# Row maxima per bank with one exponential moved last, another order in the last two steps, and the outputs' transposes taken half by half

## What is computed

```
q    = rmsnorm(rope(h @ Wq_c @ Wq_up)) ; k_sw = rmsnorm(rope(h @ Wk)) ; v_sw = h @ Wv
ck   = rmsnorm(h in blocks of 16 tokens @ W_comp)         # compressed keys, also the values
c    = softmax([mask(q ck / sqrt(D)), sink]) @ ck          # over the blocks that have ended
sw   = softmax([mask(50 tanh(q k_sw / sqrt(D) / 50)), sink]) @ v_sw   # window of 64 tokens
x1   = layernorm(h + (grouped (c + sw) @ Wg) @ Wo)
out  = layernorm(x1 + x1 @ ternary(W).T + bias)
```

## Time and profile before

| | us |
|---|---|
| Median of 3 runs | 418.98 (415.02 to 420.5) |
| The profiled execution: time | 418.8 |
| The profiled execution: span from first to last instruction | 417.0 |
| PE busy | 366.6 (88%) |
| DVE busy | 327.7 (79%) |
| POOL busy | 302.5 (73%) |
| ACT busy | 285.9 (69%) |

### The profile page before, as it was taken

One profiled execution on the slowest core, in us unless ns is written; L12 is line 12 of the kernel. 1 busy time (PEld: TensorE's weight loads), 2 busy tenths in 40 slices (PEclk: granted clock), 3 DMA queues, 4 the chain that ended last, 5 costly groups with the idle time before them and its releaser, 6 DMA issues. The chain is left out here.

```text
span 417.0 us, 8782 instructions
## 1 busy us (share of the span) xinstructions
PE 366.6 (88%) x3109; PEld 296.8 (71%) x3111; DVE 327.7 (79%) x663; ACT 285.9 (69%) x818; POOL 302.5 (73%) x190
## 2 busy tenths in 40 slices
PE   6995797958989889999999999989899999989771
PEld 5994585646859677776868787868677787868650
DVE  3686779677889998898979797999999898943411
ACT  4657764685876969696968595876969696956200
POOL 1845352074797989888979787998989898968615
PEclk9999889988999999999999999999999999999896
DMA  7993002687676775767576758787776757584350
GB/s 251 319 262 110 1 0 24 180 307 139 102 124 117 112 126 92 141 88 140 92 129 85 127 102 124 106 128 136 106 142 100 137 90 134 97 130 63 56 72 26
DMA packets 150285, 50.22 MB, mean 120 GB/s; under 512 B 138592, under 2 KB 148832, under 8 KB 149984
## 3 DMA queue, kind: packets, MB, share of 16 engines
q1 hardware_dynamic: 149424, 49.32, 63.1%
q10 hardware_dynamic: 816, 0.33, 0.3%
HBM read 11.87 MB, written 4.19 MB: 39 GB/s over the span
## 5 line engine op out<-in xcount | busy, mean ns | idle before, releaser
L1207 POOL TENSOR_TENSOR ao<-room_wg,ao 128x1024 f16<-128x1024 f32 x32 | 68.3, 2134 | 17.0 <-ACT ao L706 16.9
L666 PE MATMUL PS<-V,room_wg 128*128 128x129 f32 x512 | 69.0, 286 | 10.8 <-POOL room_wg L1217 4.5
L1217 POOL TENSOR_TENSOR room_wg<-room_comp,keep 128x1024 f32<-128x1024 f32 x32 | 74.7, 2356 | 1.9 <-ACT room_comp L822 1.9
L666 PEld LDWEIGHTS PS<-V,room_wg 128*128 128x128 f32 x512 | 62.7, 197 | 16.0 <-POOL room_wg L1217 7.0
L831 ACT ACTIVATE room_h<-PS,room_K 128x8 f32<-128x8 f32 (+7 forms) x256 | 70.8, 376 | 1.4 <-DVE room_K L1056 1.1
L831 ACT ACTIVATION_READ_ACCUMULATOR room_h<-PS,room_K 128x1 f32 x256 | 63.5, 262 | 0.0
L1223 POOL TENSOR_TENSOR ny<-nx,nu 128x16 f32<-128x16 f32 x16 | 46.7, 2916 | 22.2 <-DVE nx L1032 22.2
L632 PE MATMUL PS<-Weff,aoT 128*128 128x256 f16 x512 | 60.8, 273 | 0.4 <-DMA aoT<-ao 0.4
L632 PEld LDWEIGHTS PS<-Weff,aoT 128*128 128x128 f16 x512 | 49.8, 98 | 8.4 <-DMA aoT<-ao 1.1
L589 PE MATMUL PS<-room_h,kT 128*128 128x512 f16 x192 | 47.6, 380 | 9.2 <-DMA room_h<-room_K 8.3
L1030 DVE TENSOR_REDUCE ssq<-room_wg 128x8 f32<-128x1024 f32 x30 | 36.5, 1219 | 17.3 <-ACT room_wg L775 16.9
(11 more groups left out here) (181 smaller groups left out, 740.2 us busy)
## 6 DMA issues: line engine op xcount, KB each, us to landing
H<-in_L_attn_h SPq DMA_DIRECT2D x4, 512.0 KB, 6.3
room_wg<-in_L_attn_Wg SPq DMA_DIRECT2D x1, 2048.0 KB, 14.3
cw_rows<-staged SPq DMA_DIRECT2D x1, 2048.0 KB, 6.4
CW<-cw_rows SPq DMA_DIRECT2D x1, 2048.0 KB, 7.8
aoT<-ao SPq DMA_TRANSPOSE x128, 2.7
out<-room_wo SPq DMA_DIRECT2D x16, 128.0 KB, 2.0
CW<-in_L_attn_Wq_up SPq DMA_DIRECT2D x2, 512.0 KB, 13.1
room_wo<-in_L_attn_Wo SPq DMA_DIRECT2D x1, 1024.0 KB, 14.6
```

The costliest lines, as they stand in the source:

```text
L666: last = nc.tensor.matmul(pv, Pm[:, c, 2 * pr:2 * pr + 2, :], V[:, 2 * i + c, :], start=True, stop=True)
L1207: G.tensor_tensor(ao16[:, 1, c, :, :], ao[:, c, :, :], ao16[:, 0, c, :, :], ALU.subtract).then_inc(g_al, 1)
L1217: G.tensor_tensor(Pm[:, c, :, :], E[:, c, :, :], keep[:, :, :], ALU.mult).then_inc(g_mask, 1)
```

## The change

Four edits:

1. The compressed scores' semaphore is raised after each bank; DVE takes row maxima of one bank at a time (`row_max`), the first ahead of the first rope products, the second between the two. ACT runs only the first window exponential ahead of the sixteen compressed ones and the second behind them; each eight heads wait for their own maxima.
2. On POOL a finished tile's output moves from behind both masks to between them.
3. On SP the output transposes go high and low of the first half, then high and low of the second. For the last tile the low part of the second half is made by DVE, no longer by POOL.
4. In steps 16 and 17 PE does the CW product of tile 15 before the linear layer of tile 14, which is put between and behind the high projection; the two norms' powers are taken apart; x1 of tile 15 and the output of tile 15 are made by DVE.

The core of the diff:

```diff
@@ SP
-                wait(sp, p_cs, t)
+                wait(sp, p_cs, 2 * t)
...
-                for n, c, ready in ((0, 0, a_at), (0, 1, a_at), (1, 0, g_al), (1, 1, g_al)):
-                    sp.wait_ge(ready, 2 * i + c + 1)
+                for n, c, ready in ((0, 0, a_at), (1, 0, g_al), (0, 1, a_at), (1, 1, g_al)):
+                    if n == c == 1 and i == NT - 1:
+                        sp.wait_ge(d_al, 1)
+                    else:
+                        sp.wait_ge(ready, 2 * i + c + 1)
@@ PE
-                if ffn and not mid:
+                if ffn and not mid and not proj:
                     norm_T()
                     feed_forward()
...
-                    last.then_inc(p_cs, 1)
+                        last.then_inc(p_cs, 1)
...
                     project_blocks()
+                    if not mid:
+                        norm_T()
                     project_high(range(ahead))
+                    if not mid:
+                        feed_forward()
@@ ACT
-                    for c in range(2):
+
+                    def local_exp(c):
+
                         act.wait_ge(a_tanh, 4 * i + 2 * c + 2)
                         nc.scalar.activation(E[:, c, :, :], E[:, c, :, :], ACT.Exp, scale=CAP).then_inc(a_es, 1)
+
+                    local_exp(0)
...
-                    act.wait_ge(d_cmax, i + 1)
                     wait(act, p_ct, i)
                     n = SUB * groups(i)
                     for hd in range(HEADS):
+                        if hd % 8 == 0:
+                            act.wait_ge(d_cmax, 2 * i + hd // 8 + 1)
...
+                    local_exp(1)
@@ DVE
+                def row_max(hf):
+
+                    dve.wait_ge(p_cs, 2 * i + hf + 1)
+                    wait(dve, a_ec, 2 * i)
+                    V_.tensor_reduce(mn[:, 8 * hf:8 * hf + 8], scores(i)[:, hf, :, :], AX.X, ALU.max,
+                                     negate=True).then_inc(d_cmax, 1)
+
+                if mid:
+                    row_max(0)
                 if front:
                     rope_products(0)
                 if first:
                     weights_rest(0)
                 if mid:
-
-                    dve.wait_ge(p_cs, i + 1)
-                    wait(dve, a_ec, 2 * i)
-                    V_.tensor_reduce(mn[:, :].rearrange("p (b a) -> p b a", b=2), scores(i), AX.X, ALU.max,
-                                     negate=True).then_inc(d_cmax, 1)
+                    row_max(1)
...
+                if proj and not mid:
+                    dve.wait_ge(g_rl, NT + 1)
+                    dve.wait_ge(p_xt, NT - 1)
+                    V_.tensor_scalar(x1[:, :], y[:, :], mv[:, 0, 0:1], ny[:, HEADS:HEADS + 1], ALU.subtract,
+                                     ALU.mult).then_inc(d_x1, 1)
+                if ffn and not mid and not proj:
+                    dve.wait_ge(g_rl, NT + 2)
+                    V_.tensor_scalar(y[:, :], zs[i % 2], mv[:, 1, 0:1], ny[:, HEADS + 1:HEADS + 2], ALU.subtract,
+                                     ALU.mult).then_inc(d_out, 1)
...
+                if i == NT - 1:
+                    dve.wait_ge(a_at, 2 * NT)
+                    dve.wait_ge(s_al, 64 * i)
+                    V_.tensor_tensor(ao16[:, 1, 1, :, :], ao[:, 1, :, :], ao16[:, 0, 1, :, :], ALU.subtract).then_inc(d_al, 1)
@@ POOL
                 if mid:
-                    mask(1)
                     for tile in stored(i):
                         results(tile)
+                    mask(1)
...
+                if ffn and not mid:
+                    roots(1, 2, NT if proj else NT + 2)
+                    if proj:
+                        results(NT - 2)
+                if proj and not mid:
+                    roots(0, 1, NT + 1)
+                    pool.wait_ge(d_x1, 1)
+                    biased()
```

More of the change, by code:

```diff
@@ L1131, in step, with norms_of @@
                         weights_rest(6, 7)
+                def norms_of(sets):
+                    after_link()
+                    if sets.stop == 2:
+                        wait(dve, g_out, i - 2)
+                    for n in range(sets.start, sets.stop):
+                        chained(V_.bn_aggr(mv[:, n, :], bns[:, n, :]))
+                    after_link()
+                    V_.tensor_scalar(nx[:, HEADS + sets.start:HEADS + sets.stop], mv[:, sets, 1], 1e-5, None,
+                                     ALU.add).then_inc(d_nl, 1)
+                if ffn and not mid:
+                    norms_of(slice(1, 2))
                 if proj:
@@ L1244, in step, with roots, biased @@
                     output_low(0)
-                if proj or ffn:
-                    both = slice(HEADS if proj else HEADS + 1, HEADS + 2 if ffn else HEADS + 1)
-                    pool.wait_ge(d_nl, i)
+                def roots(first, last, done):
+                    pool.wait_ge(d_nl, done)
+                    both = slice(HEADS + first, HEADS + last)
                     G.tensor_tensor(ny[:, both], nx[:, both], nu[:, both], ALU.pow).then_inc(g_rl, 1)
-                    pool.wait_ge(g_rl, i)
-                if proj:
+                    pool.wait_ge(g_rl, done)
+                def biased():
+                    wait(pool, d_fr, i - 1)
+                    G.tensor_tensor(x1b, x1[:, :], fb_s[:, :], ALU.add).then_inc(g_xb, 1)
+                if proj and mid:
+                    roots(0, 2 if ffn else 1, i)
                     wait(pool, p_xt, i - 1)
@@ L1255, in step @@
                     pool.wait_ge(g_x1, i)
-                    wait(pool, d_fr, i - 1)
-                    G.tensor_tensor(x1b, x1[:, :], fb_s[:, :], ALU.add).then_inc(g_xb, 1)
-                if mid:
+                    biased()
+                if mid and i < NT - 1:
                     output_low(1)
-                for tile in stored(i) if not mid else ():
-                    if tile != NT - 3:
-                        results(tile)
+                if ffn and not mid:
+                    roots(1, 2, NT if proj else NT + 2)
+                    if proj:
+                        results(NT - 2)
+                if proj and not mid:
+                    roots(0, 1, NT + 1)
+                    pool.wait_ge(d_x1, 1)
+                    biased()
             all_steps(step)
```

27 lines of the change are left out of this document (12 added, 15 removed).

## The result

The changed kernel takes 432.5 us (median of 4 runs, 430.96 to 434.79). The kernel before took 417.6 us beside it (median of 4, 415.02 to 420.5). The ratio is 1.036, with a 95% interval of 1.027 to 1.045: slower. The forecast was 431, 422 to 438, and most likely slower by over 2%. Medians in this document take in every execution, while ratios and intervals leave out the few that ran in a slower state, among them one of 1257.9 us of the changed kernel with POOL's order put back, the only one of that kernel that was profiled, so that its trace isn't read.

The account below looks back on a forecast made before the run. No engine is full; tied chains through DVE, POOL and PE, with SP nearly without slack, bound the steps. 8.9 + 5.6 - 1.5 - 1.0 = +12.0 us on 418.8 gives 430.8, stated as 431 us; range 422 to 438.

Parts of the forecast that it names:

- SP's order (+8.9): Steps 1 to 3 and 9 to 11: PE's high projection waits for the sixth transpose in SP's queue; 5.15 + 3.77 us.
- 17.4 + 0.116 n: Step time in us of the loop through SP's output transposes, with n high-projection matmuls ahead: 28, 24, 20.
- upper bound (3 us more): Transposes landing 0.5 us above the median on average in steps 1 to 3 and 9 to 11: 3 us more.
- DVE's row maxima (+5.6): Wait ahead of the first reduction delays DVE 0.7 us per step, showing in steps 4 to 8 and 12 to 14.
- DVE works without a gap from L1036 to L1101: DVE's queue in a step: no idle time between these rows, so L1101 comes 0.7 us later.
- rival 2: DVE's delay is hidden because PE lets queries go out earlier; sign DVE idling ahead of L1125; +6.4, 425 us; chance 0.13.
- ACT's order (-1.5, in step 15 alone): Head exponentials start about 1 us earlier; only in step 15 are they alone on the path, 1.5 us less.
- POOL's order (0): Second mask behind the output ends about 289.9, before values(1) can start at about 290.4 in step 10: no cost.
- the cover: 0.5 us in step 10 by which POOL's second mask ends before values(1) can start on PE.
- Rival 4: POOL becomes the bound: the output's wait for the store also holds the second mask; 10 us on top, 441 us; chance 0.07.
- The last steps (-1.0): x1 and last output on DVE gain 1.5 us, a later power loses 0.5; from -3.5 to +0.5.
- no gain of the queue: Last tile's transposes: same queue of eight, low half waits for POOL, other PE work fills the time; no gain counted.

Follow-up runs that it names:

- half of SP's order: Kernel before with one of the first half's two low transposes moved ahead of the second high pair, making the last high one fifth: 426.5 us, ratio 1.017.

## Why the prediction was right, and where its steps were wrong

The total hit (431 against 432.5), the sign and the main mechanism too. Of the sum's terms only SP's and, in sign, the last steps' held; the errors of the others cancelled, and that the total hit within 2 us is luck.

**SP's order (+8.9): right in place and mechanism, sized too low.** The formula, 17.4 + 0.116 n for the steps that SP's loop holds, gave 20.65, 20.2 and 19.7 us for steps 9 to 11; measured 20.63, 20.62 and 19.90. For steps 2 and 3 it gave 20.2 and 19.7; measured 20.58 and 19.55. Step 1 took 24.10 instead of 20.65, and that is nearly all that was missing in the first six steps. Its two rows in PE's timeline:

```profile
102.96 0.68 PE L632 MATMUL PS<-CW,room_wo 112*128 112x256 f32 x2
107.34 6.02 PE L641 MATMUL PS<-Weff,aoT 128*128 128x256 f16 x28 [3.70 <-DMA aoT<-ao]
```

The same 28 matmuls take 3.23 us in step 9 (below). The granted clock explains the other 2.8, as the section on the hardware shows. The rest is a late landing: SP's eight transposes start at 96.81, the sixth was issued at 103.40, and it landed 3.9 us later, just before PE's start at 107.34. That is inside the bounds of the earlier trace rows but above their median.

The edit alone cost 13.2 us by the ratio, not 8.9. Its steps 4 to 8 took 99.83 us and 12 to 14 took 58.31, so these stayed nearly as they were, as forecast. Its steps 1 to 3 and 9 to 11 took 63.68 and 62.00, which is 3.1 and 1.45 more than the 60.55 of the formula. Landings above the median were in the prediction as an upper bound (3 us more); the low clock was not, and in step 2 of this kernel it cost 1.7 us (24 matmuls in 4.46 us instead of 2.79).

**DVE's row maxima (+5.6): wrong.** The failed step is "DVE works without a gap from L1036 to L1101", from which it followed that 0.7 us ahead of the first reduction show in eight steps. The wait was real (8.9 us in 15 times in the changed kernel) but the maxima alone cost 0.3%. DVE's chain was nearly gapless between these two rows, also in steps 4 to 8 (it had waited 0.56 and 0.35 us for PE's scores in steps 4 and 7), and the sign that was named for rival 2, DVE idling ahead of L1125 there, did not come. The slack lay ahead of L1036, where the prediction's chain began: in most of the steps in which the 0.7 us were to show DVE had waited there, and it had nothing to give in those in which they were to be hidden. Step 10 alone, from which the term was read, could not tell. It comes nearest to rival 2, by which time is won back elsewhere. What the changed kernel lost in steps 4 to 8 and 12 to 14 (3.6 us, near the 5.6 only by luck) comes from other edits; SP's and POOL's orders are the ones seen to move these steps.

**ACT's order (-1.5, in step 15 alone): wrong in sign.** I looked at what starts earlier, the head exponentials, and not at what the exponential that was moved had covered, ACT's wait for the maxima, nor at who waits for it, POOL's second mask. That order alone costs about 10 us (about 3 on top of the maxima per bank), and step 15 became 0.5 us longer instead of 1.5 shorter.

**POOL's order (0): wrong by 12 us if alone, nearly right in the sum.** The failed step is the cover: "it costs nothing, with 0.5 us". It took the store's issue at 284.25 as given, but once the second mask stands behind the store, the issue time depends on the mask, one step on. Rival 4 had named this place and priced it with 10 us, but on top of the others. On top of SP's new order it is 2 to 3 us, because that order keeps SP from standing still for the second half and so keeps the loop open. The forecast's zero was nearly right for a reason that it did not contain.

**The last steps (-1.0): right sign, too small, -2.7 measured** (34.38 to 31.47, -2.9, in the kernel with these edits alone). The row of the kernel before that the earlier trace rows don't have:

```profile
382.62 0.24 DVE L1105 RECIPROCAL room_K<-room_K 128x16 f32<-128x16 f32 x1
```

And three rows of the changed kernel's DVE:

```profile
418.90 0.48 DVE L1172 SCALAR_TENSOR_TENSOR room_wo<-PS,o_inv,H 128x256 f32<-128x256 f32 x1
...
422.24 0.41 DVE L1181 TENSOR_SCALAR room_wo<-room_wo,mv,ny 128x256 f32<-128x256 f32 x1 [1.99 <-POOL ny L1291]
...
427.42 0.41 DVE L1185 TENSOR_SCALAR room_wo<-room_f,mv,ny 128x256 f32<-128x256 f32 x1 [0.67 <-POOL ny L1291]
```

From the reciprocal of step 15 to the last sum (L1135, then L1172) it was 404.75 - 382.62 = 22.13 us and is 418.90 - 398.32 = 20.58: 1.55 less, where I had counted no gain of the queue. From there to the end of x1 it was 408.30 - 404.75 = 3.55 and is 3.75: the DVE row at 0.41 us saves 0.8 and the longer way to the power takes 1.0. From x1 to the end of the span it was 8.70 and is 7.35: 1.35 less, 0.8 of it the last output. The two DVE rows measured 0.41 us, within the bound of 0.48 that was taken.

**The signs that were named.** PE's high projection is released by the output transposes, and three steps from step 8 take 61.15 us, 60.5 forecast: right; the three from step 0 take 64.2. Each of steps 4 to 8 longer by 0.7: wrong, 1.09 in all five. PE waiting for POOL's second mask only under rival 4: it does so in three steps, 3.3 us in all, and the loop behind that rival is there in full strength as soon as SP's order is the old one.

**Of the page of the Trainium skill** ("DMA: Bandwidth & Descriptors", section "Issuing engines are not separate DMA queues"), which says that the time to start a DMA is usually small beside the DMA, so that SP's order would have cost about nothing: the runs decide against it here. One place in SP's queue cost 7 us and two cost 13, with 1.27 us for each issue.

## What to carry to other kernels

Before moving an instruction that waits for a DMA, follow what that DMA itself waits for: if the chain comes back to the instruction one step later, the wait's length in the old trace says nothing, and the loop has to be summed. When an edit that is undone alone gains nothing, undo it together with the others and compare the steps, not only the totals: here it gained 7.8 us in some steps and lost 5.9 in others, because it also held another edit's loop open. A buffer more (256 columns here) can be worth as much as an order. And when work is moved away from ahead of a wait, ask what it had covered.

## What the runs showed of the hardware

**A wait of a few microseconds can cost TensorE its clock.** PE idled 3.70 us in step 1 of the changed kernel, and the 28 matmuls behind that took 6.02 us. The same 28 in step 9:

```profile
271.28 3.23 PE L641 MATMUL PS<-Weff,aoT 128*128 128x256 f16 x28 [1.24 <-DMA aoT<-ao]
```

The windows of 100 to 110 and 110 to 120 us have a granted clock of 0.81 and 0.85 of full speed in the changed kernel (the column PEclk, third from the end), against 1.00 in both before; 6.02 against 3.23 us is near the ratio of the two levels, 1.2 and 2.4 GHz. After the changed kernel's two rows those of the kernel before:

```profile
100.00:110.00 10.00, 6.30 (x73) 4.11 (x72) 7.87 (x14) 10.00 (x41) 8.46 (x4) 0.81 0.58 85
110.00:120.00 10.00, 9.63 (x73) 8.23 (x72) 4.71 (x10) 1.35 (x3) 3.39 (x3) 0.85 0.34 64
```

```profile
100.00:110.00 10.00, 9.04 (x102) 6.29 (x101) 8.85 (x14) 10.00 (x41) 8.34 (x4) 1.00 0.68 101
110.00:120.00 10.00, 8.40 (x62) 6.78 (x61) 8.28 (x19) 6.23 (x9) 7.22 (x7) 1.00 0.73 130
```

The clock fell during the wait: the granted clock is 1.00 up to 106 us and 0.50 from 107 to 113. The waits of 1.2 and 2.0 us in steps 9 and 10 had no such effect, with 3.23 and 2.79 us for 28 and 24 matmuls. So of 16.8 us of waiting in this execution one wait cost 2.8 us more than its length.

The length of the wait alone does not decide. With SP's order alone PE idled 2.72 us in step 1 and 3.17 us in step 10, and the clock stayed at 1.00 (28 and 24 matmuls in 3.23 and 2.79 us), but behind the 2.67 us of step 2 it was 0.50 from 129 to 132 us. With half of SP's order it fell behind 2.62 us in step 1 and 2.26 us in step 12, and with the second exponential last behind 2.01 us in step 12. What tells the cases apart is open.

**Landing times vary.** A transpose lands 2.7 us after its issue in the median (2.6 to 4.7 in the changed kernel), and the sixth of step 1 after 3.9; what held it is open, no run was made on it.
